# Relation maps of both sides in one ring of four, with the logarithm and the inverse taken over two maps at once

## The reference, cut to what matters

```python
li = x @ rel_W[:, :d].T
lj = x @ rel_W[:, d:].T
logits = li[:, :, None, :] + lj[:, None, :, :] + rel_b        # [b, i, j, 3]
relation_probs = jax.nn.softmax(logits, axis=-1)
bias = jnp.einsum('bijk,hk->bhij', relation_probs, logical_bias)
attn_scores = q·k / 4 + gate * bias
attn_weights = jax.nn.softmax(attn_scores, axis=-1)
```

## Time and profile before

| | |
|---|---|
| median of 3 runs | 4449.41 us (4436.23 to 4449.67) |
| the profiled execution | 4429.6 us, its span 4427.9 us |
| mean granted TensorE clock | 0.943 |
| busy: PE | 3634.5 us (82%) |
| busy: DVE | 3607.0 us (81%) |
| busy: ACT | 3309.5 us (75%) |
| busy: POOL | 1970.2 us (44%) |

### The profile page before, as it was taken

The page is one execution under the profiler, slowest core; times in us unless marked ns, Lnnn a source line. Parts: engine busy times, 40 slices in busy tenths (PEclk is TensorE's granted clock), DMA queues, the critical chain, the costliest instruction groups (busy, mean ns, idle before and its releaser), DMA issues. The chain is left out here.

```text
span 4427.9 us, 243862 instructions
## 1 busy us (share of the span) xinstructions
PE 3634.5 (82%) x106896; PEld 2679.5 (61%) x106896; DVE 3607.0 (81%) x6310; ACT 3309.5 (75%) x3946; POOL 1970.2 (44%) x1816
## 2 busy tenths in 40 slices
PE   7548888888888888888888888989888864499991
PEld 4306666666666666666666666666666654377771
DVE  4298999999899999998999999999999623377773
ACT  2008999999899999998999999999999941244440
POOL 0014444454444455544455454555555532533335
PEclk9759999999999999999999999999999986699996
DMA  5412222222222222222222222222222252344433
GB/s 106 75 41 65 71 69 71 70 73 70 66 72 66 72 68 73 70 66 69 71 71 71 71 71 71 73 68 77 71 71 74 70 180 87 123 150 152 154 123 123
DMA packets 368338, 371.66 MB, mean 84 GB/s; under 512 B 108416, under 2 KB 342272, under 8 KB 363296
## 3 DMA queue, kind: packets, MB, share of 16 engines
q1 hardware_dynamic: 358080, 338.08, 28.0%
q0 software_dynamic: 6144, 16.79, 1.2%
q10 hardware_dynamic: 3040, 0.98, 0.1%
HBM read 99.58 MB, written 46.40 MB: 33 GB/s over the span
## 5 line engine op out<-in xcount | busy, mean ns | idle before, releaser
L716 DVE TENSOR_REDUCE b_mxp<-b_mx 128x1 f32<-128x512 f32 x4096 | 2641.2, 683 | 221.6 <-PE b_mx L833 185.1
L690 ACT ACTIVATE b_pr<-b_sc 128x1024 f32<-128x1024 f32 x2048 | 1980.1, 1019 | 319.2 <-PE b_sc L814 302.2
L856 PE MATMUL b_acc<-b_pr,vp 128*32 128x128 f32 x32768 | 1161.1, 276 | 30.6 <-issue 26.3
L856 PEld LDWEIGHTS b_acc<-b_pr,vp 128*32 128x32 f32 x32768 | 851.7, 109 | 302.7 <-issue 295.6
L802 PE MATMUL b_sc<-b_cm,b_rst 64*128 64x64 f16 x32768 | 808.9, 191 | 236.2 <-ACT b_pr L690 148.2
L833 PE MATMUL b_mx<-kst,b_qt 64*128 64x512 f16 x4096 | 818.7, 392 | 172.5 <-DVE b_mxp L716 151.3
L802 PEld LDWEIGHTS b_sc<-b_cm,b_rst 64*128 64x128 f16 x32768 | 670.2, 95 | 453.1 <-ACT b_pr L690 240.5
L613 POOL TENSOR_TENSOR b_ex<-b_ex 128x512 f32<-128x512 f32 x512 | 657.2, 1284 | 561.3 <-ACT b_ex L668 551.2
L623 POOL CAST b_rhi<-b_ex 128x512 f16<-128x512 f32 x512 | 316.5, 618 | 1069.0 <-ACT b_ex L677 764.0
L814 PE MATMUL b_sc<-b_qt,kst 64*128 64x64 f16 x32768 | 693.0, 191 | 64.5 <-issue 61.0
L814 PEld LDWEIGHTS b_sc<-b_qt,kst 64*128 64x128 f16 x32768 | 573.9, 95 | 86.8 <-issue 83.3
(11 more groups left out here) (144 smaller groups left out, 1623.1 us busy)
## 6 DMA issues: line engine op xcount, KB each, us to landing
b_rst<-b_rhi SPq DMA_DIRECT2D x1024, 128.0 KB
b_rst<-b_rlo SPq DMA_DIRECT2D x512, 128.0 KB
c_w1r<-in_L_ffn_W_dram SPq DMA_DIRECT2D x23, 1024.0 KB, 4.9
c_w2r<-in_L_ffn_W_dram SPq DMA_DIRECT2D x23, 1024.0 KB, 4.9
expert_tokens<-c_zeros SPq DMA_DIRECT2D x23, 512.0 KB, 6.7
c_xb<-expert_tokens SPq DMA_DIRECT2D x23, 512.0 KB
expert_results<-c_y SPq DMA_DIRECT2D x23, 512.0 KB, 2.8
b_qt<-q_parts SPq DMA_DIRECT2D x64, 128.0 KB
```

Of the source, the lines that this page charges most:

```text
L690: nc.scalar.activation(pr[:, jt % 2, half, :], sc[:, half].rearrange("p a b -> p (a b)"), ACT.Exp).then_inc(s["p_ready"], 1)
L716: nc.vector.tensor_reduce(mxp[:, head, part:part + 1], mx[:, (bank + ab) % MX_RING, :], AX.X, ALU.max).then_inc(s["mx_used"], 1)
L856: ins = pe.matmul(acc[32 * (h % 4):32 * (h % 4) + 32, h // 4, :], vp[:, jt, VW * h:VW * h + 32], pr[:, jt % 2, h % 2].rearrange("p (a h i) ...
```

## The change

The two slots `g % 2` of `ex` become a ring of four maps for both sides, `dl` goes, and DVE writes the clamped sums straight into `ex`, where the exponential is taken in place. ACT handles a unit in four steps: exponential of side 0, exponential of side 1, logarithm over both maps (128 x 2x512), inverse over both. It is three units ahead (six maps), where it was four maps. POOL goes by units: both sums, then the parts of both; `pool_c` moves to unit 6. DVE is four steps ahead of ACT, and waits for `lo_ready` of the map that held the slot. In the prologue the clamped sums of six maps stand with the pairs 0, 2, 4, 6, 24 and 28, and four more sums behind the pairs; the wait for all of `dj_in1` moves from behind the pairs to the fifth map, ahead of pair 24.

```diff
-R_AHEAD, D_AHEAD = 4, 3
+U_AHEAD, D_AHEAD, MAPS = 3, 4, 4
+MAP_AT = (0, 2, 4, 6, 24, 28)
-C_MAPS = (13, 14)
+C_UNIT = 6
-        dl = sb("dl", [P, 2, 2, JU])
-        ex = sb("ex", [P, 2, 2, JU])
+        ex = sb("ex", [P, MAPS, 2, JU])
...
         def pool_parts(pool, x, g):
-            pool.wait_ge(s["r_ready"], n + 1)
+            pool.wait_ge(s["r_ready"], UNITS * x + u + 1)
...
             def chunk(c, par, nth, last, slot4):      # POOL
+                for w in range(UNITS):
+                    u = w + U_AHEAD
+                    for side in range(2):
+                        if u < UNITS:
+                            pool_sum(pool, c, 2 * u + side)
+                        elif not last:
+                            pool_sum(pool, c + 1, 2 * (u - UNITS) + side)
+                    if w == C_UNIT and not last:
+                        for half in range(2):
+                            pool_c(pool, c + 1, 1 - par, nth + par, half)
+                    for side in range(2):
...
-        def act_r_exp(act, x, n):
-            act.wait_ge(s["d_ready"], 2 * g + 2)
-            if not (isinstance(g, int) and g < 2):
-                act.wait_ge(s["lo_ready"], g - 1)
-            nc.scalar.activation(ex[:, k].rearrange("p n j -> p (n j)"), dl[:, k].rearrange("p n j -> p (n j)"),
-                                 ACT.Exp).then_inc(s["e_ready"], 1)
+        def act_r_exp(act, x, g):
+            act.wait_ge(s["d_ready"], 2 * (16 * x + g) + 2)
+            both = ex[:, g % MAPS].rearrange("p n j -> p (n j)")
+            nc.scalar.activation(both, both, ACT.Exp).then_inc(s["e_ready"], 1)
+        def act_r_ln(act, x, u):
+            both = ex[:, 2 * (u % 2):2 * (u % 2) + 2, 0]
+            act.wait_ge(s["sum_ready"], 16 * x + 2 * u + 2)
+            nc.scalar.activation(both, both, ACT.Ln, bias=1.0).then_inc(s["ln_ready"], 1)
+        def act_r_inv(act, x, u):
+            both = ex[:, 2 * (u % 2):2 * (u % 2) + 2, 0]
+            act.wait_ge(s["ln_ready"], UNITS * x + u + 1)
+            nc.scalar.activation(both, both, ACT.Exp, scale=-1.0).then_inc(s["r_ready"], 1)
...
-                    g = jt // 2 + R_AHEAD
-                    if g < 2 * UNITS:
-                        (act_r_inv if jt % 2 else act_r_exp)(act, c, g)
+                    u = jt // 4 + U_AHEAD
+                    if u < UNITS:
+                        act_r_step(act, c, u, jt % 4)
...
         def dve_d(dve, x, par, nth, g, n):
-            if n == 0 and not (isinstance(x, int) and x == 0 and g < 2):
-                dve.wait_ge(s["e_ready"], 16 * x + g - 1)
-            nc.vector.tensor_scalar(dl[:, side, n], dj[:, u, n], const[:, par, side, n:n + 1], EXP_MAX, ALU.add,
+            if n == 0 and not (isinstance(x, int) and x == 0 and g < MAPS):
+                dve.wait_ge(s["lo_ready"], 16 * x + g - MAPS + 1)
+            nc.vector.tensor_scalar(ex[:, g % MAPS, n], dj[:, u, n], const[:, par, side, n:n + 1], EXP_MAX, ALU.add,
...
             for n in range(PAIRN):                    # DVE, prologue
-                if n % 2 == 0 and n < 2 * R_AHEAD:
+                if n in MAP_AT:
+                    if MAP_AT.index(n) == MAPS:
+                        dve.wait_ge(s["dj_in1"], 16 * (UNITS - 2))
                     for k in range(2):
-                        dve_d(dve, 0, 0, 1, n // 2, k)
+                        dve_d(dve, 0, 0, 1, MAP_AT.index(n), k)
                 dve_pair(dve, 0, n, 2 * n)
...
-            dve.wait_ge(s["dj_in1"], 16 * (UNITS - 2))
             for n in range(D_AHEAD):
-                dve_d(dve, 0, 0, 1, R_AHEAD + n // 2, n % 2)
+                dve_d(dve, 0, 0, 1, 2 * U_AHEAD + n // 2, n % 2)
```

More of the change, by code:

```diff
@@ L621, in pool_parts @@
             pool.sem_inc(s["pool_waited"], 1)
-            slot = 2 * (u % 2) + g % 2
-            nc.gpsimd.tensor_copy(rhi[:, slot], ex[:, g % 2, 0]).then_inc(s["hi_ready"], 1)
+            slot = g % MAPS
+            nc.gpsimd.tensor_copy(rhi[:, slot], ex[:, slot, 0]).then_inc(s["hi_ready"], 1)
             pool.wait_ge(s["hi_ready"], n + 1)
-            nc.gpsimd.tensor_tensor(rlo[:, slot], ex[:, g % 2, 0], rhi[:, slot], ALU.subtract).then_inc(s["lo_ready"], 1)
+            nc.gpsimd.tensor_tensor(rlo[:, slot], ex[:, slot, 0], rhi[:, slot], ALU.subtract).then_inc(s["lo_ready"], 1)
         @block.gpsimd
@@ L638, in _ @@
             pool.wait_ge(s["eye_made"], len(first_rows) + 1)
-            for g in range(R_AHEAD):
-                pool_sum(pool, 0, g)
-                pool_parts(pool, 0, g)
+            for u in range(U_AHEAD):
+                for side in range(2):
+                    pool_sum(pool, 0, 2 * u + side)
+                for side in range(2):
+                    pool_parts(pool, 0, 2 * u + side)
             for half in range(2):
@@ L645, in chunk @@
             def chunk(c, par, nth, last, slot4):
-                for turn in range(2 * UNITS):
-                    g = turn + R_AHEAD
-                    if g < 2 * UNITS:
[L649 to L657, removed]
@@ L659, in _ @@
-            in_chunks(pool, chunk)
-        def act_r_exp(act, x, n):
-            g, k = 16 * x + n, n % 2
-            act.wait_ge(s["d_ready"], 2 * g + 2)
-            if not (isinstance(g, int) and g < 2):
-                act.wait_ge(s["lo_ready"], g - 1)
-            nc.scalar.activation(ex[:, k].rearrange("p n j -> p (n j)"), dl[:, k].rearrange("p n j -> p (n j)"),
-                                 ACT.Exp).then_inc(s["e_ready"], 1)
[L671 to L677, removed]
+                for w in range(UNITS):
+                    u = w + U_AHEAD
+                    for side in range(2):
+                        if u < UNITS:
[5 more added lines that the diff above has]
+                            pool_c(pool, c + 1, 1 - par, nth + par, half)
+                    for side in range(2):
+                        if u < UNITS:
+                            pool_parts(pool, c, 2 * u + side)
+                        elif not last:
+                            pool_parts(pool, c + 1, 2 * (u - UNITS) + side)
@@ L679, in _, with act_r_step @@
+        def act_r_inv(act, x, u):
+            both = ex[:, 2 * (u % 2):2 * (u % 2) + 2, 0]
+            act.wait_ge(s["ln_ready"], UNITS * x + u + 1)
+            nc.scalar.activation(both, both, ACT.Exp, scale=-1.0).then_inc(s["r_ready"], 1)
+        def act_r_step(act, x, u, step):
+            if step < 2:
+                act_r_exp(act, x, 2 * u + step)
+            elif step == 2:
+                act_r_ln(act, x, u)
+            else:
+                act_r_inv(act, x, u)
         @block.scalar
@@ L681, in _ @@
             nc.scalar.preload_act_table_set("natural_log_exp_and_others")
-            for g in range(R_AHEAD):
-                act_r_exp(act, 0, g)
-                act_r_inv(act, 0, g)
+            for u in range(U_AHEAD):
+                for step in range(4):
+                    act_r_step(act, 0, u, step)
             def chunk(c, par, nth, last, slot4):
@@ L691, in chunk @@
                                              ACT.Exp).then_inc(s["p_ready"], 1)
[L692 to L694 removed]
+                    u = jt // 4 + U_AHEAD
+                    if u < UNITS:
+                        act_r_step(act, c, u, jt % 4)
                     elif not last:
[L696 removed]
+                        act_r_step(act, c + 1, u - UNITS, jt % 4)
             in_chunks(act, chunk)
@@ L768, in chunk @@
                             if slot == CLAMP_SLOT and ab == 1:
-                                g, k = R_AHEAD + (jt + D_AHEAD) // 2, (jt + D_AHEAD) % 2
+                                g, k = 2 * U_AHEAD + (jt + D_AHEAD) // 2, (jt + D_AHEAD) % 2
                                 if g < 2 * UNITS:
```

2 lines of the change are left out of this document (1 added, 1 removed).

## The result

The changed kernel takes 4528.99 us (median, 4521.72 to 4541.24), the kernel before 4444.22 us beside it: ratio 1.0181, 95% interval 1.0159 to 1.0203. That is +80 us where -10 was forecast, outside the range. The profiled execution has a span of 4520.0 us at the same granted clock (0.942, before 0.943).

The account below looks back on a forecast made before the run. No engine full, ACT and DVE level; a PE-ACT chain floors steps at 2.91 us, ACT holding only odd ones by 0.12. -43 + 0 + 4 + 29 = -10 us: 4429.6 becomes 4420, or 4440 against the median; range 4406 to 4476.

Parts of the forecast that it names:

- -43 (ACT): Attention steps: logarithm and inverse over two maps bring odd steps to the chain's floor, 43 us less, between 34 and 55.
- +4 (meetings): Attention steps: DVE's clamped sums meeting POOL's run over two maps cost 4 us more, between -6 and +8.
- +29 (prologue): Prologue: DVE's earlier wait for the key logits, and four more sums, delay the first step by 29 us, bounds 25 and 31.
- the overlay: POOL's new run laid over 249 fourth steps with their old sum starts: 22.8 us, against 19.1 in the trace as it is.
- the prediction's own rule: Attention steps: a step pays what its sum ends later than about 0.32 us after P, the start of its first exponential.
- rival B: First step behind each unit's inverse: DVE delayed by POOL's long run, +55 in place of +4, net +41, 4490; chance 0.14.
- Part 3: POOL by units: work stays the same, its place changes, meetings with DVE's sums cost +4 us.
- The floors: Attention steps: two-map relation instructions take 1.06 us each on ACT, and the chain sets calm steps at 2.91 us.
- the lower bound: Odd steps' least gain: stalls hit them as even ones, mean of max(0, 0.11 - s) is 0.066, times 508, 34 us.
- Rival C: Attention steps: PE's stalls eat the gain, odd steps gain 0.02, -10 in place of -43, net +23, 4472; chance 0.14.
- the edits costed at nothing: In-place ring of four with other waits of ACT and DVE, moved sums of exponentials, and `pool_c` earlier: each nothing.

Follow-up runs that it names:

- e1: Changed kernel with the prologue's fifth and sixth clamped sums moved from pairs 24 and 28 to 48 and 52; 4496.19 us, 1.0106 to the kernel before.
- e3: e1 with DVE's clamped sums in a unit's four steps going from 1, 1, 1, 1 to 1, 2, 1, 0; 4445.48 us, 1.0002 to the kernel before.
- e5: Kernel before with the logarithm over 352 of 512 columns; 4478.84 us, 1.0005 to the kernel before.
- e10: Kernel before with the logarithm over 64 of 512 columns; 4454.38 us, 1.0000 to the kernel before.
- e14: e10 with the hardware loop over chunks run once in place of three times; 4310.12 us, 0.9684 to the kernel before.
- e2: e1 with POOL building the next chunk's coefficients in unit 7 in place of unit 6; 4497.55 us, 1.0108 to the kernel before.
- the mended change: e1 with sums spread 1, 1, 2, 0, the third step's two in separate halves; 0.9966 to the kernel before, 0.9649 with loop run once, 0.9642 without loop.
- e16: Kernel before with all 32 chunks written out, no hardware loop; 4320.74 us, 0.9698 to the kernel before.
- e9: Kernel before, unchanged, run against itself for a profile on the same chip; 4452.34 us, 1.0009.
- e13: Kernel before with the hardware loop over chunks run once in place of three times; 4318.42 us, 0.9705 to the kernel before.

## Why the prediction was wrong

By its own terms, -43 (ACT), +4 (meetings), +29 (prologue):

- **Prologue, right.** Landing at 290.4 from the packets; DVE went on at 291.36. First step predicted at 370.6, came at 371.20. e1 brought it back by 27 us.
- **Meetings, wrong in size.** The term of +4 measured 46 (e3 against e1). The step that failed is the overlay: I put POOL's new run over the sums' old starts, one step at a time. For the step with the long run it came out. By the prediction's own rule, that a step pays what the sum ends later than 0.32 us after its P, these sums cost 20 us in the changed kernel, where I had 22.8 (in the kernel before the rule gives me 11, where I had 19.1). But a held sum makes DVE 0.3 us and more late (1433.50, a sum of 0.82 in place of 0.48), and with 2.47 us for four maxima and 0.4 for a sum DVE recovers hardly 0.1 in a step of 2.91. The next sum then meets an addition that the old starts missed, and by the same rule the sums of that step cost 31 us, before 0. All four steps together cost 55, before 14, which is near the 46 of the runs. This is rival B, which I had at 0.14 and 4490. Its mark was over 45 sums of 1.2 us or more: there are 76, before 26. (The 45 was also a slip: at 0.5 us each the net of -43 and +29 passes zero at 28 steps. And Part 3 puts the parts of a map in odd steps; the earlier trace rows has them in an even one, right behind the inverse. The window that I laid is right all the same.)
- **ACT's odd steps, wrong: the term of -43, bounded by -34 and -55, is 0.** The measured worth is nothing in the loop, at most 7 us (e5, e10), and 9 where the loop runs once (e14). The floors were right: 1.06 us for every relation instruction, and calm steps of 2.91. The step that failed is the lower bound: I took a stall to lengthen a step by itself, whatever the step before. The account that fits the runs is that an odd step's 0.1 us was the room in which PE and DVE, late from earlier steps, came level again. Take it away and the lateness shows in the next, even step: +0.061 in e10, +0.045 in e14. That the gain is a quarter in e14, where the idle time marked issue is a third, suggests that both take part. Rival C had the right result with half the mechanism. (The 34 itself used the mean of steps 4 to 23, 0.066; over all 508 even steps it is 0.059, 30 us.)
- **B and C came together.** I priced each rival alone. With C's -10, B's +55 and +29 for the prologue the sum is +74, and +80 was measured. That the differences from the changed kernel to e1 (33), from e1 to e3 (46) and from e3 to the kernel before (1) add up to 80 is no check, since they are three parts of one distance.
- Of the edits costed at nothing none shows a cost. DVE's waits on `lo_ready` are 28 us in 4 places, all in the last 36 steps, where DVE has no maxima left to do; moving the coefficients by a unit changes nothing while the meetings stand (e2).

What stays open: what PE waits for in its idle time marked issue, and whether the turns of the loop or its register instructions raise it. That DVE and PE come level again in the slack of odd steps is read from e10 and e14, where odd steps fall and even ones rise; no run isolates it. Nor does any run say where the mended change gets its 15 to 26 us from.

## What to carry to other kernels

Where three engines are within a few per cent of each other, the floor of one kind of step is not the price of that step: shortening the longer of two alternating steps can give nothing, as here, most likely since the other engines use its slack to catch up. Test the term alone with a cheap cut (a logarithm over fewer columns) before building it. And when instructions are grouped on POOL, lay the run over the other engine's starts as they will be after the first delay, not as they were.

## What the runs showed of the hardware that was not expected

- A kernel whose chunks are written out is 3.0% faster than the same chunks in a hardware loop of three turns (e16): a chunk of the first 24 takes 98.5 us in the mean, in place of 103.3 (e9). With one turn (e13) it is 98.4, and PE's idle time marked issue falls from 157 us to 54. The one-turn loop carries no register instructions either, so it doesn't tell the two apart.
- In the changed kernel 251 clamped sums start with more than 0.22 us of a POOL instruction to go, and all 251 end 0.28 us after it. The 45 that start with less than 0.18 to go take their usual 0.48. POOL is held too: an instruction of POOL that starts while a sum runs takes up to 0.32 us longer. In the mean its subtraction takes 1.192 us and the addition 1.313, before 1.161 and 1.284, over 512 each.
